# Half of the second layer's token transposes leave TensorE for VectorE and SBUF transfers, and the quantiser's steps are dealt anew

## The chip, the cores and the metric

## The reference

1024 tokens of width 512 go through two layers, each followed by a layer norm without weights:

```
x = hidden_states                                   # (2, 512, 512), float32
x = layernorm(x + attn_ref(x))     # layer 1
x = layernorm(x + ffn_ref(x))      # layer 2

attn_ref: up = x @ up_w.T ; delta = x @ gate_w.T - local_point
          out = up @ local_approx_output.T
          for m in 1..6: term = exp(log|delta|*m - discount[m-1]) * (sign(delta) if m odd) * up
                         (times |delta| <= 2.5 for m > 4);  out += term @ fuse_weight[:, :, m-1].T
          out += silu(x @ ffn_gate_w.T) * (x @ ffn_up_w.T) @ ffn_down_w.T      # 1248 wide
ffn_ref:  w1, w2, w3 are each quantised to NF4 and back: per 64 values, w / absmax goes to the nearest
          of 16 codes, and the code times absmax is used
          out = (silu(x @ dq1.T) * (x @ dq2.T)) @ dq3.T                        # 1376 wide
```

## The kernel before

Every float32 product is made of three fp32r matmuls: each operand is split in a high part (ACT copies it to fp32r: `x_hi`, `w_hi`, `l_hi`) and a low part (DVE or POOL subtracts: `x_lo`, `w_lo`, `l_lo`), and lines 1208 to 1210 multiply hi by hi, hi by lo and lo by hi. Tokens are worked on in two halves of 512 (`HALF`), or in eight tiles of 128.

The program of PE, which sets the order of everything: the up and gate products of layer 1; 20 pairs of layer 1 (`pair(1, i)`: gate and up of 128 hidden units for one half); passes 0 and 1 (`stage2`), which sum layer 1's output, four token tiles a pass in four PSUM banks, over 17 jobs (10 chunks of the down projection, 7 terms), the last jobs of a pass being run tile by tile (`stage2_end`, the tail: two jobs in pass 0, three in pass 1), which begins only when the operands of all tail jobs are ready; 22 pairs of layer 2; passes 2 and 3 for the second down projection. A job of pass 0 or 1 is 12 matmuls (4 tiles x 3). x below counts the jobs of pass 1 from 0.

Layer 2 needs its input as [feature, token], so the normalised tiles of R ([token, feature]) are transposed: `transpose_x(t)` does four 128x128 transposes on PE into PSUM bank 4 or 5 (line 1311), ACT makes `x_hi` of it (`split_x`) and DVE `x_lo` (`lo_x`, line 937). For tiles 0 to 3 this stands in pass 1 behind the jobs x = 7 and x = 9, for tiles 4 to 7 in the first two pairs of layer 2.

ACT, DVE and POOL run each its own program, written in the same order of jobs (`split_l` / `lo_of_h` / `lo_of_term` for a job's left operand are three jobs ahead, and wait until the job four before has freed the slot). Between those operations they do the NF4 quantiser of w1, w2 and w3, beside the matmuls: 17 units, each of 8 steps. In a step ACT draws a line (`side`, lines 559 and 597), POOL clamps it (`level`, line 1133), DVE adds it to the sum in PSUM (lines 825 and 829), and at a unit's end DVE multiplies by the maxima (line 832). How many steps an engine does ahead of each of its other operations stands in the table `SHARE`, one list for each engine, read one number at a time by `beside()`. `side` has 4 buffers, `level` has 3. The dequantised w1/w2 units are turned by DVE's own transpose of 32x32 squares (`turn_nf4`, line 949), since the host lays them out for that.

All semaphore waits are in order on each engine: an instruction that waits holds back everything behind it on its engine.

## Time and profile before

| | us |
|---|---|
| median of 3 runs (413.54 to 413.78) | 413.56 |
| the profiled execution | 413.98 |
| its span | 411.8 |
| PE busy in it | 403.2 |
| POOL, DVE, ACT busy | 290.7, 322.9, 265.8 |

The span is what lies between the first and the last instruction; 2.18 us of the profiled execution lie around it. In the timeline a row is an instruction or a run of equal ones (x2 and so on), with its start and its time; a matmul's time in it, 0.39 us, is longer than the distance of 0.227 us to the next one, since matmuls are pipelined. Square brackets hold the idle time of the engine ahead of the row and who ended it.

### The profile page before, as it was taken

To read this page: it belongs to the slowest core of one execution; us is meant where nothing else is said; L and a number is where in the kernel's file an instruction comes from. 1 tells how busy PE (TensorE), PEld (TensorE's weight loads), DVE (VectorE), ACT (ScalarE), POOL (GpSimd) and SP (SyncE) were. 2 spreads that over 40 slices of the span, in tenths; PEclk is the share of its full clock that TensorE was granted. 3 is DMA by queue.
4 is the path that set the end of the run, shared out by engine and by line. 5 is a ranking of instruction groups with operands and counts; after the bars stand their busy time and mean duration, and the time that the engine had idled before them with its cause. 6 is when DMAs were issued, how large, how long until landed. Compare 5 with 4: busy or idle time off the path is not lost.

```text
span 411.8 us, 5351 instructions
## 1 busy us (share of the span) xinstructions
PE 403.2 (98%) x1776; PEld 330.0 (80%) x1776; DVE 322.9 (78%) x375; ACT 265.8 (65%) x366; POOL 290.7 (71%) x228
## 2 busy tenths in 40 slices
PE   8999999999999999999999999999999999999992
PEld 7888888888877888788888888888888877888882
DVE  3629979889988976998978799986789979946025
ACT  5475677686596655456865658887778779622602
POOL 0077998979998389916993338799999979854430
PEclk9999999999999999999999999999999999999997
DMA  8993101100103442203052000000000000000202
GB/s 262 406 407 144 53 6 52 35 0 25 43 9 102 139 145 70 77 0 103 1 170 106 0 2 0 2 0 0 2 1 1 2 0 0 2 0 2 102 0 102
DMA packets 9898, 26.48 MB, mean 64 GB/s; under 512 B 1360, under 2 KB 1616, under 8 KB 9616
## 3 DMA queue, kind: packets, MB, share of 16 engines
q1 hardware_dynamic: 9872, 26.16, 18.4%
q8 instruction: 14, 0.23, 0.2%
q14 instruction: 12, 0.10, 0.1%
HBM read 24.06 MB, written 2.10 MB: 64 GB/s over the span
## 4 chain that ended last, share of the span: by engine, by line
PE 97%; DVE 2%; ACT 0%; issue 0%; POOL 0%; POOLq 0%
PE PS L1208 32%; PE PS L1209 31%; PE PS L1210 31%; PE PS L1317 2%; PE PS L1311 1%; DVE stats L907 1%; DVE R L902 0%; ACT R L663 0%; DVE mv L916 0%; POOL level L1173 0%; ACT std L656 0%; DVE std L921 0%; DVE std L924 0%; DVE std L926 0%; DVE std L927 0%
## 5 line engine op out<-in xcount | busy, mean ns | idle before, releaser
L1133 POOL TENSOR_SCALAR level<-side 128x1024 f32<-128x1024 int8 (+2 forms) x119 | 131.0, 1101 | 40.1 <-DVE PS L829 15.8
L829 DVE TENSOR_TENSOR PS<-PS,level 128x1024 f32<-128x1024 f32 (+2 forms) x102 | 120.2, 1178 | 27.3 <-POOL level L1133 23.3
L1208 PE MATMUL PS<-x_hi,w_hi 128*128 128x512 f32 (+1 forms) x352 | 137.5, 391 | 0.0
L1210 PE MATMUL PS<-x_hi,w_lo 128*128 128x512 f32 (+1 forms) x352 | 137.1, 390 | 0.0
L1209 PE MATMUL PS<-x_lo,w_hi 128*128 128x512 f32 (+1 forms) x352 | 137.0, 389 | 0.0
L559 ACT ACTIVATE side<-Q 128x1024 int8<-128x1024 f32 (+2 forms) x84 | 80.4, 997 | 16.1 <-DVE PS L825 10.6
L1163 POOL TENSOR_TENSOR l_lo<-h,l_hi 128x512 fp32r<-128x512 f32 (+1 forms) x42 | 57.6, 1379 | 29.8 <-ACT l_hi L559 28.2
L1208 PEld LDWEIGHTS PS<-x_hi,w_hi 128*128 128x128 f32 (+1 forms) x352 | 65.2, 185 | 14.8 <-issue 0.2
L1210 PEld LDWEIGHTS PS<-x_hi,w_lo 128*128 128x128 f32 (+1 forms) x352 | 65.2, 185 | 14.7
L1209 PEld LDWEIGHTS PS<-x_lo,w_hi 128*128 128x128 f32 (+1 forms) x352 | 65.3, 185 | 14.6
L1208 PE MATMUL PS<-x_hi,l_hi 128*128 128x512 f32 x144 | 56.0, 389 | 0.0
L1209 PE MATMUL PS<-x_lo,l_hi 128*128 128x512 f32 x144 | 56.0, 389 | 0.0
L1210 PE MATMUL PS<-x_hi,l_lo 128*128 128x512 f32 x144 | 56.0, 389 | 0.0
L559 ACT ACTIVATE l_hi<-h 128x512 fp32r<-128x512 f32 (+1 forms) x42 | 26.1, 628 | 29.7 <-PE PS L1210 29.7
L1152 POOL TENSOR_TENSOR w_lo<-raw,w_hi 128x1024 fp32r<-128x1024 f32 (+2 forms) x15 | 29.9, 1991 | 20.4 <-ACT w_hi L559 19.8
L559 ACT ACTIVATE side<-raw 128x1024 int8<-128x1024 f32 x35 | 35.6, 1057 | 9.4 <-DVE PS L825 6.7
L642 ACT ACTIVATE h<-PS 128x512 f32<-128x512 f32 (+1 forms) x42 | 24.8, 590 | 24.1 <-PE PS L1210 24.0
L1208 PE MATMUL PS<-w_hi,l_hi 128*128 128x512 f32 (+1 forms) x80 | 31.5, 394 | 0.0
L1208 PEld LDWEIGHTS PS<-x_hi,l_hi 128*128 128x128 f32 x144 | 27.0, 188 | 5.7
L1210 PEld LDWEIGHTS PS<-x_hi,l_lo 128*128 128x128 f32 x144 | 27.0, 188 | 5.6
L1209 PEld LDWEIGHTS PS<-x_lo,l_hi 128*128 128x128 f32 x144 | 27.0, 188 | 5.6
L1209 PE MATMUL PS<-w_lo,l_hi 128*128 128x512 f32 (+1 forms) x80 | 31.2, 391 | 0.0
(84 smaller groups left out, 501.2 us busy)
## 6 DMA issues: line engine op xcount, KB each, us to landing
Q<-w SPq DMA_DIRECT2D x10, 512.0 KB, 15.1
raw<-w_in SPq DMA_DIRECT2D x9, 512.0 KB, 11.1
raw<-w_out SPq DMA_DIRECT2D x14, 256.0 KB, 2.7
raw<-w SPq DMA_DIRECT2D x5, 512.0 KB, 3.9
R<-xN SPq DMA_DIRECT2D x2, 1024.0 KB, 6.0
out<-R SPq DMA_DIRECT2D x8, 256.0 KB, 2.0
raw<-w_fuse SPq DMA_DIRECT2D x7, 256.0 KB, 2.5
h<-xT SPq DMA_DIRECT2D x3, 512.0 KB, 6.8
```

The costliest lines, as they stand in the source:

```text
L559: return nc.scalar.activation(dst, src, ACT.Copy, **kw)
L642: nc.scalar.activation(dst, PS[0:dst.shape[0], bank, :], ACT.Silu).then_inc(s_silu, 1)
L829: v.tensor_tensor(total, total, level_of(s), ALU.add).then_inc(s_add, 1)
L907: v.bn_stats(stats[:, t, :], R[:, t, :]).then_inc(s_st, 1)
L1133: g.tensor_scalar(level_of(s), side_of(s), LIMITS[k][1], LIMITS[k][0], ALU.min, ALU.max).then_inc(s_level, 1)
L1152: g.tensor_tensor(lo, w_raw(j)[0:p, 0:n], hi.bitcast(F32), ALU.subtract).then_inc(s_wlo_in if JOBS[j][0] == "in" else s_wlo, 1)
L1163: g.tensor_tensor(lo, view, hi.bitcast(F32), ALU.subtract).then_inc(s_llo_h, 1)
L1208: t_.matmul(dst, a_hi, b_hi, start=start, stop=False)
L1209: t_.matmul(dst, a_hi, b_lo, start=False, stop=False)
L1210: return t_.matmul(dst, a_lo, b_hi, start=False, stop=stop)
L1311: last = t_.transpose(PS[:, XT_BANK + t % 2, c * P:(c + 1) * P], R[:, t, c * P:(c + 1) * P], ident[:])
L1317: last = t_.matmul(PS[:, 7, 0:2 * P], level[:, 0, 0:P], level[:, 0, P:3 * P], start=True, stop=True)
```

## The change

Tiles 0 to 3 are no longer transposed on PE. DVE transposes R's 32x32 squares in place of order (`turn_x`), SBUF to SBUF, into the first halves of chunks 0 to 3 of `h`, which layer 1 no longer reads; then SP issues 16 transfers, one for each pair of a source and a target group of 32 partitions, each of 32 partitions x 4 runs of 512 bytes (64 KB), from there into the first halves of chunks 4 to 7 of `h`. They share one semaphore, `s_xback`, and stand in SP's queue ahead of the six loads of w3. `split_x` and `lo_x` of tiles 0 to 3 read SBUF instead of PSUM, and stand four jobs later, at x = 12 and 14 instead of 8 and 10. `turn_nf4(0)` no longer waits for `x_lo` of these tiles. Tiles 4 to 7 are done as before. The three lists of `SHARE` are dealt anew from step 3 on.

```diff
     "gpsimd": [
-        0, 4, 4, 4, 2, 0, 6, 3, 9, 5, 5, 6, 4, 1, 0, 0, 0, 0, 0, 0, 1, 0, 0, 4, 0, 0, 0, 0, 4, 1, 0, 4, 0, 0,
+        0, 4, 4, 4, 2, 0, 6, 3, 7, 6, 6, 6, 4, 1, 0, 0, 0, 0, 0, 0, 1, 0, 0, 4, 1, 0, 0, 0, 7, 0, 0, 1, 0, 0,
...
+        h_first = h[:].rearrange("p (f a n) -> p f a n", f=C2, a=2)[:, :, 0, :]
+        x_squares, x_back = h_first[:, 0:TILES, :], h_first[:, TILES:2 * TILES, :]
...
+        def wait_x_turned(eng, t):
+            if t < TILES:
+                eng.wait_ge(s_xback, 16 * (P // SQ) ** 2)
+            else:
+                eng.wait_ge(s_xtr, t - TILES + 1)
...
             load_residual(1)
+            sp.wait_ge(s_xsq, TILES)
+            for q in range(P // SQ):
+                for a in range(P // SQ):
+                    sp.dma_start(x_back[q * SQ:(q + 1) * SQ, :, a * P:(a + 1) * P],
+                                 x_squares[a * SQ:(a + 1) * SQ, :, q * P:(q + 1) * P]).then_inc(s_xback, 16)
             for k in range(W3_UNITS):
...
                 beside()                                          # split_x, on ACT
-                act.wait_ge(s_xtr, t + 1)
+                wait_x_turned(act, t)
...
-                    if x in (8, 10):
-                        for t in (x - 8, x - 7):
+                    if x in (12, 14):
+                        for t in (x - 12, x - 11):
                             split_x(t)
...
+            def turn_x(t):
+                beside()
+                dve.wait_ge(s_norm, t + 1)
+                if t == 0:
+                    dve.wait_ge(s_llo_h, C1)
+                v.transpose(x_squares[:, t, :].rearrange("p (q c i) -> p c q i", q=P // SQ, c=DC),
+                            R[:, t, :].rearrange("p (c q j) -> p c q j", c=DC, q=P // SQ)).then_inc(s_xsq, 1)
...
-                if f in (0, 2):                                   # turn_nf4, on DVE
-                    dve.wait_ge(s_xl, X_PARTS + (TILES if f == 0 else TT))
+                if f == 0:
+                    dve.wait_ge(s_y, TILES)
+                elif f == 2:
+                    dve.wait_ge(s_xl, X_PARTS + TT)
...
+                    if x == 7:
+                        for t in range(TILES):
+                            turn_x(t)
-                    if x in (8, 10):
-                        for t in (x - 8, x - 7):
+                    if x in (12, 14):
+                        for t in (x - 12, x - 11):
                             lo_x(t)
...
             for n in range(PASS_START[1], PASS_START[2] - TAILS[1]):
-                x = n - PASS_START[1]
-                stage2(n, {4: (s_h, 2 * C1), 6: (s_y, 1), 7: (s_y, 2)} if x == 0 else {})
-                if x in (7, 9):
-                    transpose_x(x - 7)
-                    transpose_x(x - 6)
+                stage2(n, {4: (s_h, 2 * C1), 6: (s_y, 1), 7: (s_y, 2)} if n == PASS_START[1] else {})
```

What the dealing moves is seen in the engines' orders. First POOL, at the end of pass 0; `l_lo<-h,l_hi` are the low parts of this pass's last left operands, and the 96-row one and the one just ahead of it belong to the jobs around the tail. Before:

```order
L1133 TENSOR_SCALAR level<-side 128x1024 x3
L1163 TENSOR_TENSOR l_lo<-h,l_hi 128x512
L1152 TENSOR_TENSOR w_lo<-raw,w_hi 128x512
L1163 TENSOR_TENSOR l_lo<-h,l_hi 128x512 x2
L1163 TENSOR_TENSOR l_lo<-h,l_hi 96x512
L1133 TENSOR_SCALAR level<-side 128x1024 x3
L1124 TENSOR_TENSOR Q<-Q,rcp 128x1024
```

And of the changed kernel the same place:

```order
L1173 TENSOR_SCALAR level<-side 128x1024 x3
L1203 TENSOR_TENSOR l_lo<-h,l_hi 128x512
L1173 TENSOR_SCALAR level<-side 128x1024
L1192 TENSOR_TENSOR w_lo<-raw,w_hi 128x512
L1203 TENSOR_TENSOR l_lo<-h,l_hi 128x512 x2
L1203 TENSOR_TENSOR l_lo<-h,l_hi 96x512
L1173 TENSOR_SCALAR level<-side 128x1024 x2
L1164 TENSOR_TENSOR Q<-Q,rcp 128x1024
```

One of the three clamps that stood behind the tail's operands stands ahead of them now, and ahead of a weight's low part. (The 96-row low part is the last operand that the tail of pass 0 needs.)

Second ACT, in the jobs x = 11 to 14 of pass 1: `l_hi<-h` are the left operands of the last two jobs, `w_hi<-PS` are the turned NF4 units 0 and 1, `x_hi<-PS` or `x_hi<-h` the tokens. Before:

```order
L559 ACTIVATE l_hi<-h 128x512
L559 ACTIVATE x_hi<-raw 128x512
L559 ACTIVATE w_hi<-PS 128x1024
L559 ACTIVATE l_hi<-h 128x512
L559 ACTIVATE side<-Q 128x1024
L559 ACTIVATE w_hi<-PS 128x1024
```

And now:

```order
L586 ACTIVATE l_hi<-h 128x512
L586 ACTIVATE x_hi<-raw 128x512
L586 ACTIVATE x_hi<-h 128x4x128 x2
L586 ACTIVATE w_hi<-PS 128x1024
L586 ACTIVATE l_hi<-h 128x512
L586 ACTIVATE x_hi<-h 128x4x128 x2
L586 ACTIVATE side<-Q 128x1024
L586 ACTIVATE w_hi<-PS 128x1024
```

Two token splits, which wait for the transfers, stand ahead of the last left operand of the pass.

Third DVE, behind the norm of tiles 0 to 3 (`h<-R` is `turn_x`, `PS<-Q` `turn_nf4`, `PS<-PS,level` an added step). Before:

```order
L829 TENSOR_TENSOR PS<-PS,level 128x1024 x3
L832 TENSOR_TENSOR Q<-PS,amax 128x1024
L825 SCALAR_TENSOR_TENSOR PS<-side,level 128x1024
L937 TENSOR_TENSOR x_lo<-PS,x_hi 128x4x128 x2
L829 TENSOR_TENSOR PS<-PS,level 128x1024
```

And now:

```order
L855 TENSOR_TENSOR PS<-PS,level 128x1024
L963 STREAM_TRANSPOSE h<-R 128x4x4x32 x4
L986 STREAM_TRANSPOSE PS<-Q 128x16x2x32
L855 TENSOR_TENSOR PS<-PS,level 128x1024
L858 TENSOR_TENSOR Q<-PS,amax 128x1024
L851 SCALAR_TENSOR_TENSOR PS<-side,level 128x1024
```

Two of the adds that stood here have gone ahead, into the terms of pass 1, and one has gone behind the new transposes.

## Rows read from the trace of the kernel before

**Rows 1.** The page: each engine's busy time, and the chain that ended last.

```profile
PE 403.2 (98%) x1776; PEld 330.0 (80%) x1776; DVE 322.9 (78%) x375; ACT 265.8 (65%) x366; POOL 290.7 (71%) x228
PE 97%; DVE 2%; ACT 0%; issue 0%; POOL 0%; POOLq 0%
```

**Rows 2.** Waits of PE, whole span: engine, line, releaser, us, times, longest.

```profile
PE PS L1317 <- POOL level L1173: 1.2, 1, 1.2
```

**Rows 3.** Timeline, PE, around the transposes of tiles 0 to 3.

```profile
196.20 1.03 PE L1311 MATMUL PS<-ident,R 128*128 128x128 f32 x8
...
197.31 0.40 PE L1209 MATMUL PS<-w_lo,l_hi 128*128 128x512 f32 x1
```

**Rows 4.** Timeline, PE, into the tail of pass 0.

```profile
168.38 0.39 PE L1210 MATMUL PS<-w_hi,l_lo 128*128 128x512 f32 x1
168.80 0.47 PE L1208 MATMUL PS<-w_hi,l_hi 128*128 128x512 f32 x1
169.11 0.39 PE L1209 MATMUL PS<-w_lo,l_hi 128*128 128x512 f32 x1
```

**Rows 5.** Timeline, POOL, ahead of the same place.

```profile
157.10 3.29 POOL L1133 TENSOR_SCALAR level<-side 128x1024 f32<-128x1024 int8 x3
160.47 1.30 POOL L1163 TENSOR_TENSOR l_lo<-h,l_hi 128x512 fp32r<-128x512 f32 x1
161.72 1.30 POOL L1152 TENSOR_TENSOR w_lo<-raw,w_hi 128x512 fp32r<-128x512 f32 x1
162.98 5.68 POOL L1163 TENSOR_TENSOR l_lo<-h,l_hi 128x512 fp32r<-128x512 f32 x3
```

**Rows 6.** Timeline, DVE, beside it and elsewhere, and PE at 179.88.

```profile
147.85 0.68 DVE L1026 TENSOR_TENSOR w_lo<-raw,w_hi 128x512 fp32r<-128x512 f32 x1
...
161.93 1.64 DVE L1026 TENSOR_TENSOR w_lo<-raw,w_hi 128x512 fp32r<-128x512 f32 x1
163.49 2.33 DVE L825 SCALAR_TENSOR_TENSOR PS<-side,level 128x1024 f32<-128x1024 int8 x1
...
176.91 0.74 DVE L893 SCALAR_TENSOR_TENSOR l_lo<-h,fact,l_hi 128x512 fp32r<-128x512 f32 x1
...
179.88 0.39 PE L1208 MATMUL PS<-x_hi,l_hi 128*128 128x512 f32 x1
...
239.38 1.22 DVE L825 SCALAR_TENSOR_TENSOR PS<-side,level 128x1024 f32<-128x1024 int8 x1
```

**Rows 7.** Timeline, ACT: the side step that the moved clamp reads; the norm.

```profile
159.05 1.04 ACT L559 ACTIVATE side<-Q 128x1024 int8<-128x1024 f32 x1
...
192.93 2.94 ACT L663 ACTIVATE R<-R,std 128x512 f32<-128x512 f32 x4 [1.01 <-DVE std L928]
```

**Rows 8.** Timeline, ACT, the last left operands of pass 1.

```profile
209.15 0.63 ACT L559 ACTIVATE l_hi<-h 128x512 fp32r<-128x512 f32 x1 [0.65 <-PE PS L1210]
...
210.21 1.01 ACT L559 ACTIVATE w_hi<-PS 128x1024 fp32r<-128x1024 f32 x1
211.90 0.63 ACT L559 ACTIVATE l_hi<-h 128x512 fp32r<-128x512 f32 x1 [0.68 <-PE PS L1210]
```

**Rows 9.** Timeline, POOL and PE, into the tail of pass 1.

```profile
212.68 1.31 POOL L1163 TENSOR_TENSOR l_lo<-h,l_hi 128x512 fp32r<-128x512 f32 x1
214.35 0.39 PE L1208 MATMUL PS<-x_hi,l_hi 128*128 128x512 f32 x1
```

**Rows 10.** Groups of DVE by line: count, busy us, mean ns, idle before.

```profile
L966 DVE STREAM_TRANSPOSE PS<-raw 128x512 f32<-128x512 f32 x10 | 7.0, 714 | 0.6
```

**Rows 11.** SP's issues: by line, ns min/median/max; the page's, KB and us to landing.

```profile
L547 SPq DMA_DIRECT2D raw<-w x5: 327/328/433, 207.7 to 213.6; - x5
...
L523 SPq DMA_DIRECT2D point_sb<-point x1: 739/739/739, 4.2 to 4.2; - x1
...
out<-R SPq DMA_DIRECT2D x8, 256.0 KB, 2.0
```

**Rows 12.** A stretch: busy us of each engine, PE's clock, DMA share, GB/s.

```profile
340.00:360.00 20.00, 20.00 (x89) 15.89 (x88) 19.07 (x27) 15.54 (x28) 18.12 (x19) 1.00 0.00 1
```

More of the change, by code:

```diff
@@ L353, in build @@
         s_norm_last = sem("s_norm_last")
+        s_xsq, s_xback = sem("s_xsq"), sem("s_xback")
         s_xtr, s_turn, s_w3turn = sem("s_xtr"), sem("s_turn"), sem("s_w3turn")
@@ L444, in build, with x_turned, x_part @@
         XT_BANK = 4
+        def x_turned(t):
+            if t < TILES:
+                return x_back[:, t, :].rearrange("p (a c i) -> p c a i", a=P // SQ, c=DC)
+            return PS[:, XT_BANK + t % 2, :].rearrange("p (c a i) -> p c a i", c=DC, a=P // SQ)
+        def x_part(x, t):
+            return x[:, :, t * P:(t + 1) * P].rearrange("p c (a i) -> p c a i", i=SQ)
+        def wait_x_turned(eng, t):
+            if t < TILES:
+                eng.wait_ge(s_xback, 16 * (P // SQ) ** 2)
+            else:
+                eng.wait_ge(s_xtr, t - TILES + 1)
         def w3_bank(c):
@@ L672, in split_x @@
                     act.wait_ge(s_tile, TT)
-                copy(x_hi[:, :, t * P:(t + 1) * P],
-                     PS[:, XT_BANK + t % 2, :].rearrange("p (c t) -> p c t", c=DC)).then_inc(s_xh, 1)
+                copy(x_part(x_hi, t), x_turned(t)).then_inc(s_xh, 1)
             def split_nf4(f):
@@ L936, in lo_x @@
                     dve.wait_ge(s_tile, TT)
-                v.tensor_tensor(x_lo[:, :, t * P:(t + 1) * P],
-                                PS[:, XT_BANK + t % 2, :].rearrange("p (c t) -> p c t", c=DC),
-                                x_hi[:, :, t * P:(t + 1) * P].bitcast(F32), ALU.subtract).then_inc(s_xl, 1)
+                v.tensor_tensor(x_part(x_lo, t), x_turned(t), x_part(x_hi, t).bitcast(F32),
+                                ALU.subtract).then_inc(s_xl, 1)
             def turn_nf4(f):
@@ L1307, in transpose_x @@
                     pe.wait_ge(s_xl, X_PARTS + t - 1)
-                elif t >= TILES:
+                else:
                     pe.wait_ge(s_wlo4, 2)
```

24 rows, old and new, of the table SHARE are left out of this document.

## The prediction

> **What bounds the kernel now.** I read the page first: PE is busy 403.2 of 411.8 us, and 97% of the chain that ended last is PE [rows 1]. Then PE's waits: over the whole span the profile names one, 1.2 us ahead of the warm-up matmuls [rows 2]. So PE is the bound, end to end, and the time is the sum of its instructions and of the few moments in which it stands still. What must be looked at is how close the others come to making it stand still, and that no list of waits shows. I read it from the timelines: distances between PE's matmuls that are longer than the usual 0.227 us, and, where an operand is handed over, how long before its use it was ready. Three places matter here. At the tail of pass 0, two matmuls that are 0.45 us apart elsewhere take 168.38 to 169.11, so 0.28 us are lost, though the list of waits has no row for it [rows 4]; the last operand of that tail, the third of three low parts on POOL, ended at 162.98 + 5.68 = 168.66, 0.14 us ahead of the matmul at 168.80 [rows 4, 5]. At the tail of pass 1 the last low part ends at 213.99 and PE takes it at 214.35: 0.36 us in hand [rows 9]. Everything else has over a microsecond in hand, or is a time that follows PE itself.
>
> **What is removed from PE.** Eight of the sixteen transposes of two tiles stand in one row: from 196.20 to the second matmul behind it are 1.11 us, of which one matmul distance, 0.23, remains without them; 0.88 us go [rows 3]. There are two such groups in pass 1 and both read alike: -1.76 us. Nothing covers them, PE is the bound. That is the whole gain that the change can have by itself; the waits that hung on them (PE for the norm, ACT for the transposes) had slack and give nothing.
>
> **What is added on others.** DVE gets four square transposes of 128x512, 0.71 us each by its transposes of w3 [rows 10], so 2.9 us in a stretch in which it waits for the norm anyway; ACT and DVE have as many token splits as before, four jobs later; SP gets 16 issues. The splits of tiles 0 to 3 are needed by the first pair of layer 2, some 10 us after they stand in the new order, so by themselves they cost nothing. What counts is what they and the dealt steps are put in front of.
>
> **Term 1, the tail of pass 0.** POOL is gapless here: 157.10 to 168.66, row to row [rows 5]. The new order puts one more clamp ahead of the last four operations. Its own inputs are ready (its side step ends at 160.09 [rows 7]), so it runs, and it costs at least 3.29 / 3 = 1.10 us. It can cost more, since DVE and POOL hold each other up: a low part of a weight on DVE takes 0.68 us at 147.85 and 1.64 at 161.93, the first step's add 1.22 at 239.38 and 2.33 at 163.49, and POOL's three low parts take 5.68 instead of 3 x 1.25 = 3.75 (1.25 is the distance from 160.47 to 161.72) [rows 5, 6]. The durations fit turns: who comes second waits for the other's operation, then runs alone. I laid out the new order by such turns: clamp 161.8 to 162.9, DVE's weight to 163.5, POOL's weight to 164.75, DVE's first add to 165.95, first low part to 167.2, DVE's second weight to 167.8, second low part to 169.05, DVE's product of the terms (it has one more add in front of it now, and so arrives here) to 169.65, third low part to 170.9. PE would be ready at 168.53 and starts 0.14 after the operand: 171.04, a stand of 2.51 instead of 0.28. That is +2.2 us. From below: +1.1, the bare clamp. From above: the same turns, set 0.45 us later by two low parts of DVE that the new order also moves together at 148: +2.7. I take +2.2, since the row it is nearest to, the 5.68 us, shows the turns at work.
>
> The Trainium skill, "SBUF — State Buffer", section "Who interferes with whom", says that a VectorE instruction with both inputs in SBUF contends with a GpSimd instruction that reads SBUF, and the second to issue blocks until the first is through. The rows just read agree (1.64 against 0.68 us); by its rule the sum is what the turns give, +2.2, and by bare durations it would be +1.1.
>
> **Term 2, the terms of pass 1.** Three adds, 1.22 us each, go ahead of DVE's low part of the third term, which ended at 176.91 + 0.74 = 177.65 and is used at 179.88, 2.2 us later [rows 6]. Ahead of it DVE has little idle time. 3.5 us more against 2.2 of slack, to which term 1 adds its 2.2: between 0 and 0.7 us, the latter if it must also let a clamp through. I take 0.2.
>
> **Term 3, the tail of pass 1.** Everything here hangs on the end of PE's job x = 11, and moves with it, so I work in the times of before. ACT took the left operand at 209.15, the raw copy, then the NF4 unit at 210.21, and the last left operand at 211.90, by its own wait for PE [rows 8]. Now two token splits stand between. They have 128x512 elements like the two copies from 209.15 to 210.21, so I give them the same 1.06 us: the last left operand starts at 210.21 + 1.06 + 1.01 = 212.28 at the earliest, 0.38 later. POOL's low part follows 0.78 behind it and takes 1.31 [rows 8, 9]: from 213.06 to 214.37. With 0.14 for the hand-over, as in pass 0, PE goes on at 214.51 instead of 214.35: a stand of 0.16 us. Here too the turns come in: DVE's `x_lo` now reads both inputs from SBUF and falls between POOL's last two operations, 0.6 us more each time ((5.68 - 3.75) / 3). From 0.15 to 0.9; I take 0.6.
>
> **The transfers.** The norm of tiles 0 to 3 ended at 195.87 [rows 7]; with 2.2 of term 1 that is 198.1, the fourth transpose ends at 198.8. An issue takes 0.33 us [rows 11] and 0.05 to the next: 16 of them end at 204.9, and 2.0 us is the shortest landing on the page [rows 11]: 206.9. ACT's first token split comes at 210.2 (behind the raw copy of rows 8) - 1.76 + 2.2 + 0.2 = 210.8. So 3.9 us in hand, cost nothing. The loads of w3 behind them wait for a split at 207.7 anyway [rows 11].
>
> **The sum.** -1.76 + 2.2 + 0.2 + 0.6 = +1.24. The profiled execution took 413.98, so 415.2; the median of the runs lies 0.42 below it, at 413.56: **414.8**. The likeliest case's own range, with the ends of the three terms: -1.76 + 1.1 + 0 + 0.15 = -0.5 to -1.76 + 2.7 + 0.7 + 0.9 = +2.5, 413.0 to 416.1.
>
> **Rivals.** *The clean gain (not slower).* POOL's turns with DVE fall differently, since both have a new order. If none of the blocks hit, the five operations end at 161.77 + 1.10 + 4 x 1.25 = 167.9, ahead of PE's 168.53: then the 0.28 us go too, and 413.56 - 1.76 - 0.28 = 411.5, or 411.8 with a trifle at pass 1. It decides at 168.4: every tenth that the third low part is later is a tenth lost. For it: the same three low parts take 1.25 us when DVE reads PSUM. Against it: DVE's two weights and its first add stand where they stood.
>
> *The transfers are late.* The trace has no transfer from SBUF to SBUF. If an issue of 128 short runs costs what the slowest small one did, 0.74 [rows 11], 16 last 11.8 us and land at 198.8 + 11.8 + 2.0 = 212.6 or later, 1.8 us behind ACT's wait at 210.8, and the last left operand of pass 1, on which the whole tail hangs, stands behind that wait: 414.8 + 1.8 = 416.6. Against it: every issue with full rows takes 0.33 to 0.43.
>
> The Trainium skill, "DMA: Bandwidth & Descriptors", section "Bandwidth", gives 0.95 us for 64 KB and calls transfers under 64 KB descriptor-dominated. By an estimate from that page 16 in a row would last 15.2 us and put the time near 420; no row here shows such a transfer.
>
> *The late steps.* From 255 to 345 us POOL is dealt three to five steps fewer ahead of each product than before, and makes up for them by 357. DVE is busy 19.07 of the 20 us from 340 to 360 [rows 12]; four more adds are 4 x 1.22 = 4.9 us there, and what the low parts of the last w3 chunks have in hand against them no row shows. If they have 3.4, PE waits for 1.5 us: 416.3. Against it: PE is busy all 20 us there, and a microsecond of idle DVE is left.
>
> **Chances.** The forecast's case 58%, the clean gain 18%, late transfers 10%, late steps 14%. To tell from no change takes about 0.2%, 0.8 us, here: 412.7 to 414.4. The clean gain and a little of the forecast's low end are faster: 20%. Of the forecast's own range the part below 414.4 is the same: 20%. Slower: 60%. Two in ten may fall outside: most of the clean gain's and of the late transfers' ends. Range 411.8 to 416.8.
>
> **What would show it.** Right: PE's distance of 0.42 us at 168.4 has grown to 1.3 to 2.9, with POOL's third low part ending just before PE goes on; the transposes' rows on PE are down to 16; PE stands once more, under 1 us, at the tail of pass 1; the last of the 16 transfers lands before ACT's `x_hi<-h` wants to start, so that ACT waits for PE and not for a DMA. Wrong: PE goes through the tail of pass 0 without a stand (then the turns are no fixed matter, and the time is near 411.6); ACT's `x_hi<-h` is released by a DMA; or PE waits at 340 to 360, where I see none.

## The result, and the profile after

The changed kernel takes 419.39 us (median of 4 runs, 418.71 to 420.10) against 413.55 of the kernel before in the same session: ratio 1.0142, 95% interval 1.0129 to 1.0154. The prediction was 414.8 us with a range to 416.8; the direction was right, the size was not. The profiled execution took 418.71 us, its span is 416.9.

The page of the changed kernel: busy times, and the chain that ended last by engine, as in [rows 1].

```profile
PE 402.0 (96%) x1760; PEld 326.6 (78%) x1760; DVE 327.2 (78%) x379; ACT 264.6 (63%) x366; POOL 293.5 (70%) x228
...
PE 79%; DVE 6%; issue 5%; POOL 4%; ACT 2%; DMA 2%; SPq 0%; POOLq 0%; DVEq 0%; ACTq 0%
```

PE has 16 instructions fewer and is busy 1.2 us less, but only 79% of the chain is PE's now: it stands. Its waits (engine, line, releaser, us, times, longest), where [rows 2] had one:

```profile
PE PS L1248 <- POOL l_lo L1203: 2.2, 4, 0.8
PE PS L1248 <- DVE x_lo L1031: 1.7, 2, 1.0
PE PS L1248 <- ACT Q L586: 1.5, 1, 1.5
PE PS L1357 <- POOL level L1213: 1.2, 1, 1.2
PE PS L1248 <- DVE R L928: 0.9, 1, 0.9
```

Where these are, PE's timeline shows (the last matmul ahead of each stand and the first behind it):

```profile
166.56 0.39 PE L1250 MATMUL PS<-w_hi,l_lo 128*128 128x512 f32 x1
167.72 0.47 PE L1248 MATMUL PS<-w_hi,l_hi 128*128 128x512 f32 x1 [0.76 <-POOL l_lo L1203]
...
170.30 0.39 PE L1250 MATMUL PS<-w_hi,l_lo 128*128 128x512 f32 x1
171.35 0.47 PE L1248 MATMUL PS<-w_hi,l_hi 128*128 128x512 f32 x1 [0.67 <-POOL l_lo L1203]
...
214.90 0.39 PE L1250 MATMUL PS<-w_hi,l_lo 128*128 128x512 f32 x1
215.75 0.47 PE L1248 MATMUL PS<-x_hi,l_hi 128*128 128x512 f32 x1 [0.47 <-POOL l_lo L1203]
...
223.78 0.39 PE L1250 MATMUL PS<-x_hi,l_lo 128*128 128x512 f32 x1
225.07 0.47 PE L1248 MATMUL PS<-x_hi,w_hi 128*128 128x512 f32 x1 [0.91 <-DVE R L928]
...
237.75 0.40 PE L1250 MATMUL PS<-x_hi,w_lo 128*128 128x512 f32 x1
239.65 0.47 PE L1248 MATMUL PS<-x_hi,w_hi 128*128 128x512 f32 x1 [1.50 <-ACT Q L586]
```

The first three are at the places that the prediction named (two at the tail of pass 0, one at that of pass 1). The last two, at the first and second pair of layer 2, are not in it, and they are the larger part. The wait that is put down to `ACT Q` is in fact one for `x_lo` of the last tile, which DVE ended at 239.50.

A sum that adds up is had by laying PE's matmuls of the two traces side by side, number by number (the transposes left out), and reading how far the one lies behind the other. The changed kernel against the one before, in us that each stage adds: start +0.62; around 150 us +0.33; tail of pass 0 +1.65; the two groups of removed transposes -1.79; tail of pass 1 +0.72; first pair of layer 2 +1.16; second pair +1.93; around 355 us +0.55; together +5.1, the difference of the spans. The start is scatter: over all kernels below it lies between -0.5 and +0.6. At 150 and 355 us the stands are too short for a bracket or just long enough for one; both are taken up below.

The two late stands begin at one place, in DVE and POOL from 209 to 224 us. DVE:

```profile
211.62 5.98 DVE L973 TENSOR_TENSOR x_lo<-h,x_hi 128x512 fp32r<-128x512 f32 x2 [3.25 <-ACT x_hi L586]
217.53 1.21 DVE L995 TENSOR_TENSOR w_lo<-PS,w_hi 128x1024 fp32r<-128x1024 f32 x1
...
220.01 2.47 DVE L973 TENSOR_TENSOR x_lo<-h,x_hi 128x512 fp32r<-128x512 f32 x2
...
223.54 1.27 DVE L928 TENSOR_TENSOR R<-PS,R 128x512 f32<-128x512 f32 x2
```

and POOL beside it:

```profile
210.57 1.28 POOL L1192 TENSOR_TENSOR x_lo<-raw,x_hi 128x512 fp32r<-128x512 f32 x1
211.82 1.28 POOL L1203 TENSOR_TENSOR l_lo<-h,l_hi 128x512 fp32r<-128x512 f32 x1
213.07 1.29 POOL L1192 TENSOR_TENSOR x_lo<-raw,x_hi 128x512 fp32r<-128x512 f32 x1
214.33 1.28 POOL L1203 TENSOR_TENSOR l_lo<-h,l_hi 128x512 fp32r<-128x512 f32 x1
```

Two `x_lo` of tiles 0 to 3 take 5.98 us; before, out of PSUM, two took 1.28. POOL's operations keep their 1.28 us. So here the two engines do not take turns: DVE's first `x_lo` starts at 211.62 and ends at 216.16, half a microsecond after POOL's run is over at 215.61: three operations of POOL that started after it went ahead of it. Behind it on DVE stands the norm of tiles 4 to 7, whose first step, `R<-PS`, starts at 223.54 instead of 217.43. (In x3 below, where `x_lo` is short, it starts at 218.23 and waits for PE.)

### The profile page after: what moved, and what is told of

Its sections match the earlier page's. It is cut to its first block, busy times and chain, and to the rows that moved or that the text cites. A ratio compares the mean times of both kernels' runs of the same rounds, so it can differ in the third digit from the quotient of the medians.

```text
span 416.9 us, 5338 instructions
## 1 busy us (share of the span) xinstructions
PE 402.0 (96%) x1760; PEld 326.6 (78%) x1760; DVE 327.2 (78%) x379; ACT 264.6 (63%) x366; POOL 293.5 (70%) x228
## 4 chain that ended last, share of the span: by engine, by line
PE 79%; DVE 6%; issue 5%; POOL 4%; ACT 2%; DMA 2%; SPq 0%; POOLq 0%; DVEq 0%; ACTq 0%
PE PS L1248 26%; PE PS L1250 26%; PE PS L1249 26%; POOL l_lo L1203 2%; DMA h<-xT 2%; POOL level L1173 1%; DVE stats L933 1%; DVE R L928 1%; ACT x_hi L586 1%; DVE x_lo L973 1%; DVE PS L855 1%; DVE w_lo L995 1%; DVE PS L851 1%; ACT Q L586 0%; ACT R L690 0%
## 5 line engine op out<-in xcount | busy, mean ns | idle before, releaser
L1210 POOL TENSOR_TENSOR h<-h,Q 128x512 f32<-128x512 f32 (+1 forms) x22 | 30.3, 1376 | 10.2 <-ACT Q L586 9.0
```

The costliest lines, as they stand in the source:

```text
L1210: g.tensor_tensor(dst, dst, up2[0:dst.shape[0], k % 2, :], ALU.mult).then_inc(s_h2, 1)
```

## The experiments

All tables of steps not spoken of are the changed kernel's. "The lists of before" means: as many steps ahead of each operation as in the kernel before. The table has PE's delay against the kernel before, by stage, from each kernel's trace as above (`tail0` and `tail1` are the tails of the two passes, `terms` the jobs around 180 us, `transp` the stretch of the removed transposes, `pair0` and `pair1` the first and second pair of layer 2), and the ratio of the medians to the kernel before in the same session with its 95% interval.

```
kernel  start  ~150  tail0  terms  transp  tail1  pair0  pair1  ~355   sum  median  ratio (interval)
after    0.62  0.33   1.65   0.00   -1.79   0.72   1.16   1.93  0.55   5.1  419.39  1.0142 (1.0129 to 1.0154)
x1      -0.22  0.00  -0.26  -0.02    2.55   1.83   0.00   0.00  0.06   4.0  417.72  1.0103 (1.0089 to 1.0117)
x2      -0.18  2.20   0.70  -0.02    0.00   9.06   0.10   0.00  0.53  12.3  426.29  1.0323 (1.0297 to 1.0349)
x3      -0.25  2.21   0.71   0.00   -1.79   0.74   0.00   0.00  0.51   2.1  415.15  1.0041 (1.0029 to 1.0054)
x4      -0.01  0.00   0.00   0.00    1.15   3.87   0.06   2.05  0.00   7.1  420.74  1.0176 (1.0162 to 1.0190)
x5       0.05  2.22   0.71   0.00   -1.79   0.74   0.00   3.47  0.49   5.8  418.94  1.0140 (1.0127 to 1.0154)
x6       0.07  0.00   0.01   0.82   -1.79   0.83   1.15   1.87  0.51   3.5  416.58  1.0074 (1.0052 to 1.0095)
x7      -0.16  0.00   0.01   0.83   -1.79   0.82   0.00   3.48  0.51   3.7  417.22  1.0099 (1.0086 to 1.0112)
x8       0.38  0.00   0.01   0.85   -1.79   0.80   0.00   4.58  0.06   4.9  418.19  1.0118 (1.0103 to 1.0132)
x9      -0.46  0.00  -0.27   0.83   -1.79   0.76   0.00   2.49  0.06   1.6  415.30  1.0051 (1.0038 to 1.0064)
x10     -0.32  0.00   0.02   2.70   -1.66   2.07   0.00   2.46  0.06   5.3  418.88  1.0136 (1.0122 to 1.0152)
x11      0.17  0.36   1.61   0.00   -1.79   0.70   1.18   1.88  0.57   4.6  416.94  1.0086 (1.0071 to 1.0101)
x12      0.18  0.36  -0.16   0.84   -1.79   0.83   1.22   1.81  0.58   3.8  418.17  1.0111 (1.0073 to 1.0149)
x13      0.09  0.00   0.01   0.85   -1.79   0.82   0.00   0.78  0.55   1.3  414.41  1.0020 (1.0012 to 1.0029)
x14      0.11  0.00  -0.27   0.83   -1.79   0.03   4.71   2.27  0.06   6.0  419.41  1.0139 (1.0126 to 1.0152)
x15      0.04  0.00   0.01   0.29   -1.68   4.98   3.35   2.16  0.00   9.1  422.71  1.0217 (1.0204 to 1.0230)
x16     -0.47  0.00   0.01   0.81   -1.79   0.84   0.00   1.89  0.06   1.4  415.08  1.0035 (1.0022 to 1.0047)
x17     -0.28  0.00  -0.26   0.26   -1.69   3.57   0.11   0.31  0.00   2.0  416.03  1.0056 (1.0043 to 1.0070)
```

**The stage at 150 us, read from the traces.** The changed kernel's lists put DVE's low part of a term (line 919) behind the two maxima of a quantiser unit, and PE waits for it. Before, that operation ran from 142.97 to 143.71 and nobody waited. DVE in the changed kernel, and PE behind it (idle for 0.07 us by the trace, but 0.46 instead of 0.23 behind the matmul ahead):

```profile
146.91 0.18 DVE L821 TENSOR_SCALAR rcp<-amax 128x32 f32<-128x32 f32 x1
...
148.51 1.71 DVE L919 SCALAR_TENSOR_TENSOR l_lo<-h,fact,l_hi 128x512 fp32r<-128x512 f32 x1
```

```profile
150.37 0.47 PE L1248 MATMUL PS<-x_hi,l_hi 128*128 128x512 f32 x1
```

The stage has two sizes. x2, x3 and x5 have the same lists up to here, and 2.2 us where the changed kernel, x11 and x12 have 0.33 to 0.36. DVE in x3:

```profile
146.05 1.33 DVE L821 TENSOR_SCALAR rcp<-amax 128x32 f32<-128x32 f32 x1
...
148.80 2.42 DVE L919 SCALAR_TENSOR_TENSOR l_lo<-h,fact,l_hi 128x512 fp32r<-128x512 f32 x1
```

In all six traces the small operation and a low part on POOL start within 0.01 us of each other. In three of them it takes 0.18 us. In the other three it takes 1.33 and ends 0.04 behind POOL's, and DVE's low part then meets POOL's product of 1.9 us instead of a low part of 1.3. The tail of pass 0 gives a part back (0.71 for 1.65), so that pass 0 costs 1.98 us in the changed kernel's trace and 2.9 in those of x2, x3 and x5.

**Code and dealing apart (x1, x2).** In x1 the three lists become those of before (zero ahead of the new and moved operations); x2 is the kernel before with the lists of the changed one.

```diff
-        0, 4, 4, 4, 2, 0, 6, 3, 7, 6, 6, 6, 4, 1, 0, 0, 0, 0, 0, 0, 1, 0, 0, 4, 1, 0, 0, 0, 7, 0, 0, 1, 0, 0,
+        0, 4, 4, 4, 2, 0, 6, 3, 9, 5, 5, 6, 4, 1, 0, 0, 0, 0, 0, 0, 1, 0, 0, 4, 0, 0, 0, 0, 4, 1, 0, 4, 0, 0,
```

> The changed kernel's code (squares on DVE, 16 transfers, splits four jobs later) with the step lists of before: ahead of each operation stand as many steps as before, and none ahead of the moved splits. Theory A, read from the traces of before and after: two costs of different origin. The dealt steps cost the 1.75 us at the tail of pass 0 and about 0.7 us at 150 and 352 us; the code itself costs 3 us at 224 and 238 us, because DVE's x_lo of tiles 0 to 3 now reads both inputs from SBUF and is held by POOL (5.98 us for two instead of 1.28), and the norm of tiles 4 to 7 stands behind it. Then this kernel takes 419.4 - 1.75 - 0.7 = 417.0 us, with no stand over 0.4 us at the tail of pass 0, and stands of some 1.1 and 1.7 us near 223 and 237. Theory B, the dealt steps are all of it: 413.55 - 1.76 = 411.8 us.

> The kernel before with the step lists of the changed kernel: tokens still transposed on PE, splits at x = 8 and 10; one of DVE's steps stands ahead of its first x_lo, since the engines wait for each other otherwise. Theory A: the tail of pass 0 stands 1.75 us longer than before, 0.2 at 150, 0.5 at 352, nothing near 224 and 238: 413.55 + 2.45 = 416.0 us. Theory B, the dealt steps are all of it: 419.4 + 1.76 = 421 us. Rival C, the dealt steps only cost together with the new code: 413.6.

x1 came out near the number of theory A (417.72 for 417.0) and at other places, so it does not support it: no stand at the pairs, but 4.3 us at 201 (the 2.55 under `transp` is this less 1.79) and 1.8 at the tail of pass 1. At 201, DVE's adds, which freed POOL's clamps ahead of a low part, now stood behind the four `turn_x` and these behind the norm. x2 was 10 us off, most of it in two waits of PE for POOL's `l_lo`, 1.9 us at 213.55 and 3.6 at 224.46, and in what follows such waits. The lists are no property of the machine that can be carried between the two codes; each fits its own order, and "deal" and "code" can't be told apart by exchanging them whole. What x1 does show is what a long stand can cost beyond itself. PE in x1 behind the stand, and PE in windows of a microsecond (the columns are PE's busy time, its granted clock, DMA share, GB/s):

```profile
201.27 0.77 PE L1251 MATMUL PS<-w_hi,l_hi 128*128 128x512 f32 x1 [2.69 <-POOL l_lo L1206]
...
202.26 0.63 PE L1253 MATMUL PS<-w_hi,l_lo 128*128 128x512 f32 x1
...
204.30 0.39 PE L1252 MATMUL PS<-w_lo,l_hi 128*128 128x512 f32 x1
```

```profile
202.00:203.00 1.00, 1.00 (x4) 0.50 0.51 121
...
205.00:206.00 1.00, 1.00 (x6) 1.00 0.33 77
```

Between two matmuls that start 3.07 us apart (198.20 and 201.27) the granted clock falls to half, the 1.2 GHz level, and stays there for some three microseconds, in which matmuls stand 0.43 us apart instead of 0.23. That adds about 1.4 us to the stand. None of the stands in the changed kernel does this: behind each only the next distance is 0.31 instead of 0.23. The length of the stand alone does not decide it: a distance of 2.20 us in x17 (212.15 to 214.35) was followed by half clock from 215 to 218.4, ones of 2.33 in x5 (149.33) and 3.05 in x8 (232.28) were not. The stages of x2, x4, x14, x15 and x17 that come to over 3.3 us each hold such a stretch.

**The x_lo and POOL (x3 to x9).** x3 changes one input, so that these low parts hold other values (and DVE waits for its own last add, in whose bank it reads):

```diff
-                v.tensor_tensor(x_part(x_lo, t), x_turned(t), x_part(x_hi, t).bitcast(F32),
+                v.tensor_tensor(x_part(x_lo, t), x_psum(t), x_part(x_hi, t).bitcast(F32),
```

> The changed kernel, but DVE's x_lo of tiles 0 to 3 takes its first input from a PSUM bank (6 or 7, in which the sums of the quantiser lie) and not from the turned tokens in SBUF, so these low parts hold other values; sizes, order and waits are the same. Theory A (POOL holds DVE when both inputs come from SBUF): each x_lo takes 0.65 to 0.7 us instead of up to 4.54, the norm of tiles 4 to 7 comes 4 us earlier, the stands near 223 and 237 go: 419.4 - 2.9 = 416.5 us. Rival (the order of DVE's work at x = 12 to 14 is too long by itself): 419 to 419.4, the two stands stay.

Both stands at the pairs went, 3.09 us to 0.00, and the median fell by 4.2 us. (In the traces the whole fell by 3.0, since x3's has the larger of the two sizes in pass 0.) The group of these operations in the changed kernel and in x3 (ns min/median/max):

```profile
L973 DVE TENSOR_TENSOR x_lo<-h,x_hi x4: 1028/1522/4539, 211.6 to 221.0; 128x512 fp32r<-128x512 f32 x4
```

```profile
L977 DVE TENSOR_TENSOR x_lo<-PS,x_hi x4: 668/676/691, 211.7 to 216.2; 128x512 fp32r<-128x512 f32 x4
```

This is the main finding: same engine, place and size, and one input in PSUM makes 0.68 us of up to 4.54. x5 gives the four operations to POOL, x6 undoes the dealing up to the end of pass 0, x7 does both:

```diff
-                    if x in (12, 14):
-                        for t in (x - 12, x - 11):
-                            lo_x(t)
...
+            for t in range(TILES):
+                beside()
+                pool.wait_ge(s_xh, X_PARTS + t + 1)
+                wait_job_done(pool, PLACE[1, ("fuse", 3)])
+                g.tensor_tensor(x_part(x_lo, t), x_turned(t), x_part(x_hi, t).bitcast(F32),
+                                ALU.subtract).then_inc(s_xlp, 1)
```

> The changed kernel with its own step lists; only x_lo of tiles 0 to 3 is made by POOL behind its last low part of pass 1, with one clamp (on which DVE's next add waits) ahead of it. The first run with POOL's x_lo (with the lists of before) missed because POOL came to the next clamp at 222.6 only and DVE's add and norm waited for it; that is taken away here. Theory A (DVE held by POOL at x_lo costs the stands at 225 and 239 us): both go, 419.4 - 2.9 = 416.5 us. Rival (the stands come from when PE ends the pass, not from x_lo): 419 us or more.

> The changed kernel with the step lists of before up to the end of pass 0, and its own from there on: the clamp stands behind the tail's operands again. Theory A: the stands at 150 and at the tail of pass 0 (2.2 us in the changed kernel's profile, 0.28 before) shrink to 0.28, the stands at 215, 225 and 239 us stay: 419.4 - 1.9 = 417.5 us. Rival (the blocks between DVE and POOL fall anew and give it back later): 419 us, with a larger stand at the tail of pass 1.

> The two edits together: step lists of before up to the end of pass 0, and x_lo of tiles 0 to 3 on POOL with one clamp ahead. Theory A, the costs add: 419.4 - 1.9 - 2.9 = 414.6 us; left are 0.28 at pass 0, 0.7 at the tail of pass 1 and 0.5 at 357. Rival (one hides the other): 416 us.

x6 met its number nearly (-2.8 us by the medians, -1.6 in the traces, against -1.9 expected): pass 0 goes through as before, and 0.82 us of the second term, hidden so far behind the stands of pass 0, come up. x5 and x7 missed. The stand at the first pair went, but the one at the second pair grew from 1.9 to 3.5 us. ACT in x5:

```profile
224.10 1.15 ACT L628 ACTIVATE side<-Q,line 128x1024 int8<-128x1024 f32 x1 [7.03 <-POOL Q L1162]
```

POOL came 5 us later to the product that this side step reads, and ACT's root for the norm stood behind the side step. x4, an earlier form of it with the lists of before, had met the same on DVE (6.5 us for a clamp) and the hold-up of x1 besides, and was 8.8 us off; x8 is x7 with the lists of before also from the first pair on.

> The changed kernel's code with the step lists of before, and x_lo of tiles 0 to 3 made by POOL behind its last low part of pass 1, not by DVE: 4 x 1.29 = 5.2 us there, ahead of a stretch in which POOL was idle for 7.6 us. Theory A: DVE's norm is no longer held up, POOL has them at about 219.5, ahead of the first pair at 221: only the 0.28 us of before stay, 413.55 - 1.76 + 0.1 = 411.9 us. Rival: POOL's operations and those of DVE's norm hold each other up, or POOL's clamps come too late: 413.5 or more, with a stand at the first or second pair of layer 2.

> As the kernel just before, but the step lists of before also from the first pair of layer 2 on, so that only those of pass 1 are the changed kernel's. Theory A: the stand of 0.5 us at 357 goes too: 414.1 us; if the tail of pass 1 is through without a stand, 413.4, below the kernel before. Rival (with fewer steps done in pass 1 than in the lists of before, POOL comes late in the pairs): 415 us or more.

In x8 the 0.5 us at 355 went, so that part is the dealing's; the total missed by 4 us for the same reason as x7, and the second pair costs 1.1 us more than in x7 (4.58 for 3.48), as the rival had it. x9 is x8 with ACT's side steps dealt out behind the root (a row of `"scalar"`):

```diff
-        2, 0, 0, 0, 0, 0, 0, 0, 0, 0, 0, 0, 0, 0, 0, 2, 0, 1, 0, 0, 0, 0, 0, 0, 0, 1, 3, 0, 0, 0, 0, 0, 1, 0,
+        2, 0, 0, 0, 0, 0, 0, 0, 0, 0, 0, 0, 0, 0, 0, 2, 0, 1, 0, 0, 0, 0, 0, 0, 0, 1, 0, 0, 1, 1, 1, 0, 0, 1,
```

> As the kernel with only pass 1 dealt anew and x_lo on POOL (418.2 us), but ACT's four side steps that stood ahead of its first root in the norm of tiles 4 to 7 stand behind it, one by one. In the kernels with x_lo on POOL the stand at 225 us went, but the one at the second pair grew to 3.5 to 4.6 us: ACT waited 7 us for POOL's Q (now behind the four x_lo) with the norm's root behind that wait. Theory: then that stand goes altogether, 418.2 - 4.5 = 413.7 us. Rival (POOL's x_lo makes DVE's adds late by itself): 416 us or more.

2.1 of 4.6 us went, the rest stayed. The reason is on DVE, beside POOL's four `x_lo`, the product and the two clamps behind them (214.38 to 223.53):

```profile
219.96 1.35 DVE L951 TENSOR_SCALAR std<-mv 128x2 f32<-128x2 f32 x1
...
221.77 0.64 DVE L955 TENSOR_TENSOR std<-std 128x2 f32<-128x2 f32 x1
...
222.65 0.89 DVE L957 SCALAR_TENSOR_TENSOR std<-std 128x2 f32<-128x2 f32 x1
```

```profile
214.38 5.04 POOL L1235 TENSOR_TENSOR x_lo<-h,x_hi 128x512 fp32r<-128x512 f32 x4
219.37 1.91 POOL L1162 TENSOR_TENSOR Q<-Q,rcp 128x1024 f32<-128x1024 f32 x1
221.36 2.17 POOL L1171 TENSOR_SCALAR level<-side 128x1024 f32<-128x1024 int8 x2
```

Operations on two numbers a partition, 0.16 to 0.17 us elsewhere, take 0.64 to 1.35 here, and each ends 0.01 to 0.02 us behind the operation that POOL had under way: the product first, then the two clamps. So the subtraction costs on either engine here.

**One clamp; behind the run (x12, x13).** x12 moves the one clamp of the prediction's first term, and its add, back:

```diff
-        0, 4, 4, 4, 2, 0, 6, 3, 7, 6, 6, 6, 4, 1, 0, 0, 0, 0, 0, 0, 1, 0, 0, 4, 1, 0, 0, 0, 7, 0, 0, 1, 0, 0,
+        0, 4, 4, 4, 2, 0, 6, 3, 7, 6, 6, 6, 4, 1, 0, 0, 0, 0, 0, 0, 1, 0, 0, 4, 0, 0, 0, 0, 8, 0, 0, 1, 0, 0,
```

> The changed kernel, with only the one clamp on POOL (and DVE's add that waits for it) moved back behind the operands of pass 0's tail. The prediction's first term: the stands at the tail of pass 0 shrink from 1.9 us to 0.3, the rest stays: 419.4 - 1.6 = 417.8 us. Rival (the place at 150 us, where two low parts of DVE were moved together, sets it): 419 us, with 0.7 us or more left at the tail.

The tail of pass 0 went from +1.65 to -0.16 us. POOL in the changed kernel, with the clamp, and in x12 without:

```profile
162.60 1.05 POOL L1173 TENSOR_SCALAR level<-side 128x1024 f32<-128x1024 int8 x1
163.72 1.62 POOL L1192 TENSOR_TENSOR w_lo<-raw,w_hi 128x512 fp32r<-128x512 f32 x1
165.31 5.90 POOL L1203 TENSOR_TENSOR l_lo<-h,l_hi 128x512 fp32r<-128x512 f32 x3
```

```profile
162.04 1.29 POOL L1195 TENSOR_TENSOR w_lo<-raw,w_hi 128x512 fp32r<-128x512 f32 x1
163.30 5.68 POOL L1206 TENSOR_TENSOR l_lo<-h,l_hi 128x512 fp32r<-128x512 f32 x3
```

x12's executions spread from 414.9 to 420.8 us, so its verdict rests on the trace, not on the median. The 0.36 us at 150 stay in x12 and go in x6: they are no part of what the clamp costs. x13 is x6 with DVE's `x_lo` moved behind the operations on the NF4 units:

```diff
-                    if x in (12, 14):
-                        for t in (x - 12, x - 11):
-                            lo_x(t)
                     if x == 10:
                         turn_nf4(0)
                     if x in (12, 14):
                         lo_nf4((x - 12) // 2)
                         if x == 12:
                             turn_nf4(1)
+                    if x in (12, 14):
+                        for t in (x - 12, x - 11):
+                            lo_x(t)
```

> The kernel with pass 0 undone (416.6 us, profiled 417.0), with one more edit: DVE's x_lo of tiles 0 and 1 stand behind the low part of NF4 unit 0 and the turn of unit 1, those of tiles 2 and 3 behind the low part of unit 1. They start some 4 us later, when POOL's gapless run of low parts is over. Theory A (POOL's run holds DVE): the two pairs of x_lo take some 2.5 us each and not 6, the norm starts 1.8 us earlier, the stands at the first and second pair shrink from 3.0 us to 1.2 or less: 415.0 us or less. Rival (they cost the same anywhere): 416.6 to 417.

It took 414.41 us, and the stands at the pairs are 0.78 in sum instead of 3.02. DVE in x13, where POOL's run ends at 214.05:

```profile
213.92 2.12 DVE L976 TENSOR_TENSOR x_lo<-h,x_hi 128x512 fp32r<-128x512 f32 x2
...
217.10 2.70 DVE L976 TENSOR_TENSOR x_lo<-h,x_hi 128x512 fp32r<-128x512 f32 x2
...
219.72 1.27 DVE L931 TENSOR_TENSOR R<-PS,R 128x512 f32<-128x512 f32 x2
```

One `x_lo` costs 0.67 to 1.53 us there, beside POOL's single operations, and not 4.5.

**The tail of pass 1, and the rest (x14 to x17, x10, x11).** x14 is x13 with the lists of before from the first pair on, and with one clamp (2.03 us in the changed kernel, at 202.18) taken out of POOL's run ahead of the tail of pass 1; its add goes too, and ACT's `x_hi` stay where they are. x15 is x14 with DVE's three adds spread over the terms; x16 is x13 with the lists of before from the first pair on, x17 is x16 with the spread adds; x10 was a first try of the spread on x9, with the four `x_hi` behind the last left operand. The edits are moves in the lists: first x14's clamp (`"gpsimd"`, the first number; the rest of the line is that of before), then the spread (`"vector"`, x17 against x16).

```diff
-        1, 0, 0, 0, 0, 0, 0, 0, 0, 5, 2, 1, 2, 2, 2, 2, 2, 5, 0, 3, 0, 0, 0, 2, 4, 2, 3, 3, 2, 5, 1, 3, 5, 2,
+        0, 0, 0, 0, 0, 0, 0, 0, 0, 8, 2, 0, 2, 3, 1, 3, 5, 3, 0, 0, 0, 4, 0, 1, 4, 4, 1, 2, 5, 3, 1, 6, 2, 3,
...
-        0, 0, 0, 0, 0, 0, 0, 1, 1, 3, 2, 0, 0, 0, 0, 2, 0, 0, 2, 0, 0, 0, 0, 0, 0, 0, 0, 0, 0, 0, 0, 0, 0, 0,
+        0, 0, 0, 0, 0, 0, 0, 1, 1, 3, 2, 0, 0, 0, 0, 0, 0, 0, 1, 0, 1, 0, 0, 0, 1, 0, 0, 0, 1, 0, 0, 0, 0, 0,
```

> As x13, and one clamp (2.03 us in the changed kernel, amid the gapless run of POOL ahead of the tail of pass 1) with its add stands behind that tail; from the first pair of layer 2 on the step lists are those of before. Theory: the 0.8 us at the tail of pass 1 are POOL's pace (it is gapless from 198 us on, and PE comes 1.76 us earlier than before), and go, the 0.5 at 357 too: 1.3 us less than x13, 413.7 us. Rival (ACT's x_hi ahead of the last left operand, as the prediction had it): the stand at the tail of pass 1 stays at 0.6 or more.

> As x14, and DVE's three added steps of pass 1 stand ahead of one low part each, with ACT's steps there as before. Expected: the 0.8 us at 180 us shrink to 0.3: 413.2 us, level with before or just below. Rival (as in the first try of this edit, later adds hold clamps, side steps and with them ACT's left operands): 415 us or more, with stands at 185 to 190.

> As x13, with the step lists of before from the first pair of layer 2 on. Theory: only the 0.5 us at 357 go: 414.4 - 0.5 = 413.9 us. Rival (fewer steps done in pass 1 make the pairs late): 415 or more, with a larger stand at the second pair.

> As x16, and the three added steps of DVE stand ahead of one low part each, with ACT's steps there as before; POOL's run and DVE's scales stay. Theory: 0.85 us at 180 shrink to 0.3: 413.3 us, just below before. Rival (the norm of tiles 0 to 3 comes later, and with it the transfers and the last left operands): a stand of 2 us or more at the tail of pass 1, 416 us.

> The kernel just before with two more edits: the four x_hi of tiles 0 to 3 stand behind the last left operand of pass 1 on ACT, not two ahead of it, and the three adds that were all ahead of the low part of the third term stand ahead of one low part each. Theory: the stand at the tail of pass 1 (0.8 us) and that at 180 us (0.8) go or shrink to 0.3 in sum, and the gain of the removed transposes is left: 413.7 - 1.3 = 412.4 us, below the 413.1 to 413.6 of before. Rival (the stand at the tail of pass 1 is POOL's own pace, not ACT's x_hi): 413.2 to 413.7 us.

x14's tail of pass 1 fell from 0.82 to 0.03 us as expected: it was POOL's gapless run. Its total missed by 5.7 us, since with the step went the maxima of the next units, which on DVE (216.06 to 218.13) now stood ahead of the norm: it started at 223.76, in x13 at 219.72. x15 was 9.5 us off, with waits of PE for POOL's `l_lo` at the tail of pass 1 (3.3 us) and for the norm at the first pair (2.2).

x16 lost the 0.5 us at 355 and got 1.1 at the second pair back; its median is 0.7 us above x13's. x17 took the stand at 180 down to 0.26 and paid 3.57 at the tail of pass 1. POOL's gapless run ended at 214.20 there, in x13 at 214.05; PE, which came 1.1 us earlier, stood that much longer (1.8 us) and then ran at half clock. Its rival had the time (416.03 for 416) but not the reason: ACT did wait 0.65 us for a transfer at 208.97, but the last left operand was ready at 211.56 and POOL took it at 212.95. x10 shows how such a spread comes back, first on ACT, then on DVE:

```profile
184.14 1.06 ACT L590 ACTIVATE side<-Q 128x1024 int8<-128x1024 f32 x1 [2.17 <-POOL level L1171]
```

```profile
185.84 0.75 DVE L923 SCALAR_TENSOR_TENSOR l_lo<-h,fact,l_hi 128x512 fp32r<-128x512 f32 x1 [2.94 <-ACT l_hi L590]
```

A later add holds a clamp, the clamp a side step, and the term's left operand stands behind the side step. No version beats the kernel before; x13 comes nearest.

x11 has no transfers:

```diff
-                eng.wait_ge(s_xback, 16 * (P // SQ) ** 2)
+                eng.wait_ge(s_xsq, TILES)
```

> The changed kernel without its 16 transfers: ACT and DVE read the squares that DVE has turned, in their first place, so tiles 0 to 3 hold other values in layer 2; all other work and its order is the same. Theory A (the transfers land just ahead of their use and cost nothing): 418.7 to 420.1 us, as the changed kernel, with the same stands. Rival (ACT's x_hi and with it the last left operand of pass 1 hang on the last transfer): 418.6 us or less, with no stand at 215 us.

Its profiled execution has every stand of the changed kernel to 0.1 us, that at 215 included, so in the traced execution the transfers cost nothing. Its median is 2.4 us lower all the same, and its executions range from 415.9 to 418.2, the traced one being the slowest; all of them are faster than the fastest of the changed kernel, 418.71. What its other executions did is not known.

## Why the prediction was wrong, step by step

**The removed transposes**: -1.76 predicted, -1.79 measured, in each kernel that has neither a stand among them nor the terms spread. Right.

**Term 1, the tail of pass 0**: +2.2 predicted, +1.65 measured; x12 shows that the one clamp makes it (1.81 us between the two traces, for an operation of 1.05). Right, by the turns of DVE and POOL: the clamp made the operations behind it longer as well, 1.62 us for the weight's low part and 5.90 for the three, against 1.29 and 5.68 in x12. PE's distance did not grow to 1.3 to 2.9 us at one place, as the sign had it, but to 1.16 and 1.05 at two, since the first of the three low parts was late too. The 0.33 us at 150 are another cost, at a place where the prediction saw a delay of 0.45 in DVE's work and no stand of PE; that term and stage together come to 1.98, near the 2.2, is luck, since in x2, x3 and x5 the same lists gave 2.9.

**Term 2**: 0.2 predicted of 0 to 0.7. In the changed kernel 0, behind the stands of pass 0, as the working had it (3.5 us of adds against 2.2 of slack and 2.2 of term 1). Where the stands of the tail are gone (x6 to x9, x12 to x14, x16) the three adds cost 0.81 to 0.85; by the same working it would be 1.3.

**Term 3, the tail of pass 1**: +0.6 predicted, +0.72 measured, and the reason given was wrong. ACT's last left operand started at 212.93 and was ready at 213.54; POOL took it at 214.33, out of a run with no gap over 0.1 us since 198.29. The prediction asked only when the operand would be ready (ACT), and not that POOL's run, 0.36 us ahead of PE before, would be overtaken once PE came 1.76 us earlier. The 0.78 us that it read between ACT's operand and POOL's low part was no lag behind ACT: before, too, POOL came out of such a run. The row ahead of POOL's in [rows 9]:

```profile
211.43 1.31 POOL L1152 TENSOR_TENSOR x_lo<-raw,x_hi 128x512 fp32r<-128x512 f32 x1
```

x14, with the two `x_hi` in place and the run shorter by a clamp, has 0.03, and x17 shows the run's end standing still while PE comes earlier. That 0.72 lies near the 0.6 is luck.

**The transfers**: no cost in the trace, as predicted, but with 0.7 us in hand and not 3.9. SP's issues in the changed kernel and ACT's first split:

```profile
198.46 10.41 SPq L565 DMA_DIRECT2D h<-h  x16
```

```profile
210.98 1.14 ACT L586 ACTIVATE x_hi<-h 128x512 fp32r<-128x512 f32 x2
```

16 issues at 0.65 us a piece, not 0.38; the last one started at 208.27 and landed at 210.32. (The 2.0 us of landing count from the start of an issue, so the prediction's sum holds one issue too many.) The nearest row was one of large transfers; the slowest small one, 0.74, taken as the rival's price, was nearer.

**The step that failed** is the sentence "so by themselves they cost nothing" on the splits of tiles 0 to 3. It weighed when `x_lo` is needed and not what it holds up while it runs: +3.09 us at the two pairs, more than half of the whole. The fact was at hand, since term 3 says that `x_lo` now reads both inputs from SBUF and meets POOL; but it put the delay on POOL and took it to be one turn, 0.6 us. It fell on DVE, lasted through three of POOL's operations, and the norm of tiles 4 to 7 stood behind it. x3 shows the cause, x13 shows that the place makes the size. With it the sum of the prediction's kind comes out: -1.79 + 1.65 + 0 + 0.72 for its own terms is +0.6, and 3.09 at the pairs, 0.33 at 150, 0.55 at 355 and 0.62 of scatter at the start bring it to 5.2, which is the +5.1 but for rounding.

The Trainium skill, "SBUF — State Buffer", section "Who interferes with whom", says that whoever issues second blocks until the first is through. In pass 0 the traces agree; at 211.62 they show more, a block through three operations in a row (4.54 us), which by that sentence would have been one.

**The late steps**: the forecast had nothing here, the rival 1.5 us; measured +0.55. It is the dealing, since x8, x14 and x16 with the lists of before there have 0.06, but not by the rival's path. PE goes on at 357.44, behind a wait of 0.27 us for POOL's low part of a left operand and not for DVE's of w3, and POOL makes it behind two clamps:

```profile
353.76 2.17 POOL L1173 TENSOR_SCALAR level<-side 128x1024 f32<-128x1024 int8 x2
356.01 2.55 POOL L1203 TENSOR_TENSOR l_lo<-h,l_hi 128x512 fp32r<-128x512 f32 x2
```

**Left open.** Only one execution of each kernel has a trace, and the others differ from it: the changed kernel's median lies 0.7 us above the traced execution, x11's 1.3 below it, x12's six executions lie between 414.9 and 420.8. What follows is argued, not shown. Two places are known to have two sizes. With the larger one in pass 0 the traced 418.71 would be 419.65, near the slower executions of 419.86 and 420.10. And `x_lo` is blocked through POOL's run in four traces (the changed kernel, x6, x11, x12: 4.52 to 4.62 us) but takes turns with it in one (x1: 1.00 and 1.79, with POOL's operations at 1.74); in x6, where the block costs 3.0 us, executions of 414.3 and 415.1 stand beside ones of 417.1. A rival stays for the 2.4 us between x11 and the changed kernel: transfers that land later than the traced ones, which had 0.7 us in hand. Neither explains x12's 420.8. Nor is it shown what decides between a turn and a block; in the four traces DVE came 0.97 to 1.06 us after the start of POOL's operation, in x1 0.84 after it.

## What to carry to other kernels

Work that is moved off the bounding engine is priced by what stands behind it on its new engine, also where its result is needed late; look at where its inputs lie and what the neighbour that shares their path does at that time. When the bound gets faster, look for chains that have kept just ahead of it: a gapless run of another engine with 0.4 us in hand is the next bound, whatever the operands' times say. A table that deals steps between engines fits one order of work; exchanged whole it costs more than what it was to test. And where two engines reach a shared path within 0.01 us of each other, as at 146 us here, one trace does not price the place: look at several kernels that have it.

## What the hardware showed that was not expected

- A subtraction of 128x512 on DVE with both inputs in SBUF took 0.67 us at its shortest (x13), 1.0 to 1.8 beside other operations of POOL, and 4.52 to 4.62 beside a gapless run of four in four traces, three of which POOL started after it; with one input in PSUM 0.67 to 0.69 beside the same run (x3).
- Three operations of DVE on 128x2 took 0.64 to 1.35 us instead of 0.16 to 0.17 (x9), each until POOL's operation under way was over, a product or a clamp. One on 128x32 took 0.18 or 1.33, with starts of the two engines within 0.01 us (six traces).
- An issue of an SBUF-to-SBUF transfer of 32 partitions x 4 runs of 512 bytes took 0.60 us of SP (0.59 to 0.74), 0.65 from one to the next, and it landed 2.0 after its start.
- A distance of 3.07 us between two matmuls (x1) was followed by three microseconds at half clock, worth 1.4 us, and so was one of 2.20 (x17); ones of up to 1.9 us in the changed kernel, 2.33 in x5 and 3.05 in x8 were not.
